# First attention: the weighted sum over the first key tile in three split passes, with half of the next queries in front of it

## The chip, the core and the metric

The kernel runs on one core of a Trainium2 chip. The metric is the time of one execution on the device in microseconds, as the median of several runs. The core has a matrix engine (PE, TensorE), a vector engine (DVE, VectorE), a scalar engine (ACT, ScalarE) and a general one (POOL, GpSimd). Each works off its own queue of instructions in order and waits for the others by semaphores. PE writes into PSUM, of which this kernel uses eight banks of 512 columns.

## What is computed

A block of six layers on x, 1024 tokens by 512: half a gated feed-forward layer, an attention, the same feed-forward layer again, then a low-rank feed-forward layer, a second attention and the low-rank layer again, each behind a layer norm and added to x. The change concerns the first attention. For each of 4 batches of 256 tokens it has 32 heads of width 128; a head's query is used twice, once on a key that four heads share and once on a latent key of its own:

```
q  = rope(x @ w_q)                 # 32 heads
k  = repeat(rope(x @ w_k), 4);  v  = repeat(x @ w_v, 4)
lk = rope((x @ w_lq) @ w_lk);   lv = x @ w_lv
attn = softmax(causal(q k^T * scale)) v
lat  = softmax(causal(q lk^T * scale)) lv
x = x + attn @ w_o + lat @ w_lo
```

All of it is in float32. The kernel gets float32's precision out of a reduced format (F32R) that PE reads faster: an operand is stored as a HI part, rounded to that format, and a LO part, the rest, and a product is made of three passes, HI x HI, HI x LO and LO x HI.

## The kernel before

`product` (L357 is its matmul) issues the three passes. A plain float32 matmul (both operands F32) is one instruction in the source and appears in the trace as two records, each with its own weight load.

The first attention runs over 8 groups of heads (one shared key each), and in a group over 16 steps: 4 batches of 4 query heads. A step handles two "instances": k = 0, the head on the shared key, and k = 1, the head on its latent key. That makes 128 steps and 256 instances. The groups 0 to 6 are a hardware loop, whose body starts with the step numbered 2; the last group is written out, without products for a next one. A step mixes three stages: the scores of step s, the turning and the weighted sum of step s-1, and the output product of step s-2. In it:

- PE (`a0_tensor_step`): `turn(0)` transposes the probabilities of instance 0 into bank PT (three blocks of 128x128: keys of tile 0 by queries of tile 0, keys of tile 0 by queries of tile 1, keys of tile 1 by queries of tile 1; the causal fourth block is empty). `scores` of both instances. In each third step of a batch (`st.key`) the next batch's keys. `weigh(0)`, the weighted sum into bank OB: a matmul over the first key tile for all 256 queries, and one over the second key tile for the last 128. `turn(1)`. `a0_queries`: twelve matmuls of 256 columns for the queries of two steps on, and three for their latent keys. `output(0)`: six matmuls of 512 columns. `weigh(1)`, `output(1)`. In each first step of a batch `a0_values` follows, 48 matmuls of 320 columns, four products of twelve.
- ACT (`a0_scalar_step`): `turned_out(0)` copies PT to `pt0` (L1086), the HI part of the last rotated query (L1070), the exponentials of both instances (L1079), `result_hi(0)` (the HI part of OB, L1091), `turned_out(1)`, HI parts of weight chunks (L256), the half swap of the queries for rope (L1064, L1065), `result_hi(1)`. In a key step the keys' swap stands between the exponentials of instance 0 and those of 1.
- DVE (`a0_vector_step`): the rotation of the last query (L1179, adds the cosine and the sine part), the row minima of both instances out of the scores' banks (L1191 for 128 columns, L1193 for 256), the inverses of the row sums (L1201), in a key step the key's cosine (L1170) and rotation, `result_lo(0)` (the LO part of OB, L1206), LO parts of weight chunks (L262), the queries' cosine (L1170), `result_lo(1)`, the output added to x (L1248, in each second step of a batch), and behind the values their four copies to `lvv` (L1213).
- POOL (`a0_gpsimd_step`): LO parts of the rotated queries and keys (L1286), the scaling of the probabilities by the inverses (L1297, L1299), the sine part of rope (L1278).

`weigh` waits until `a_pt` tells that its probabilities are in `pt0`, and until `a_o_lo` tells that OB has been emptied. `a0_claim` waits until the bank of a projection (two, in turn) has been released through `a_proj_free`.

Of the kernel before, what the change touches and what calls it, by code (L numbers as in the profile page):

```python
# [133 lines left out]
def program(nc, x_in, w_in, table_in, bias_in, rows_in, out):  # L134
    ctx = ExitStack()
    with ctx:
# [27 lines left out]
        with ExitStack() as a:  # L164
            xnB = [sb(a, f"xnB{i}", [P, KC, CH], F32R) for i in (HI, LO)]
            with ExitStack() as s:
                WF0 = [sb(s, f"WF0_{i}", [P, F0_CHUNKS * CH], F32R) for i in (HI, LO)]
                h0 = [sb(s, f"h0_{i}", [P, 2, CH], F32R) for i in (HI, LO)]
            with ExitStack() as s:

                qk = [sb(s, f"qk{i}", [P, 6, SEQ], F32R) for i in (HI, LO)]
                lvv = sb(s, "lvv", [P, 2, LVW])
                pt0 = sb(s, "pt0", [P, 2, 3 * P])
                oT0 = [sb(s, f"oT0_{i}", [P, 4, SEQ], F32R) for i in (HI, LO)]
                lqT = [sb(s, f"lqT{i}", [P, TOKENS], F32R) for i in (HI, LO)]
                s0 = sb(s, "s0", [P, 4, 3 * P])
                normed = sb(s, "normed", [P, 4, DIM])
# [597 lines left out]
        a_turned = sem("a_turned")  # L775
        a_pt = sem("a_pt")
        a_pv = sem("a_pv")
# [138 lines left out]
        def a0_queries(pe, st):  # L916

            dst, to = a0_claim(pe, st, "q"), st.near(2)
            for c in range(KC):
                w = (C_Q + to.h) * CH + c * P  # L920
                product(dst[:, 0:SEQ], lambda p: W[p][:, w:w + P],
                        lambda p: xn(p, c, to.tokens), c == 0, c == KC - 1)
            w = C_LK * CH + to.h * P
            product(dst[:, SEQ:2 * SEQ], lambda p: W[p][:, w:w + P],
                    lambda p: lqT[p][:, to.tokens]).then_inc(a_proj, 1)
# [17 lines left out]
        def a0_tensor_step(pe, st):  # L943
# [21 lines left out]
            def weigh(k):  # L965
# [3 lines left out]
                if before.h == 0 and k == 0:  # L969
# [102 lines left out]
        def a0_scalar_step(act, st):  # L1072
# [11 lines left out]
            def turned_out(k):  # L1084
                act.wait_ge(a_turned, before.inst(k)[0] + 1)
                nc.scalar.copy(pt0[:, k, :], bank[PT][:, 0:3 * P]).then_inc(a_pt, 1)  # L1086
# [13 lines left out]
            if st.key:  # L1100
                a0_swap(act, st, "k")
            if st.heads:
# [79 lines left out]
        def a0_vector_step(dve, st):  # L1182
# [25 lines left out]

            def values(i):
                tt, half = divmod(i, 2)  # L1210
                f, fs = st.fill(i)
                dve.wait_ge(a_proj, f + 1)
                nc.vector.tensor_copy(lvv[:, tt, half * HALF:(half + 1) * HALF],  # L1213
                                      bank[fs][:, 0:HALF]).then_inc(a_proj_free, 1)
# [9 lines left out]
            if st.first:  # L1224
                a0_cosine(dve, st, "q")
                values(0)
            if st.heads:
                inverses(0)
# [769 lines left out]
```

## Time and profile before

| | us |
|---|---|
| median of 3 runs | 1891.56 (1889.14 to 1893.09) |
| the profiled execution | 1892.9 |
| its span in the trace | 1891.1 |
| PE busy in the span | 1765.6 (93%) |
| DVE busy | 1124.1 (59%) |
| ACT busy | 1086.6 (57%) |
| POOL busy | 906.7 (48%) |

The steps of the first attention begin near 100 us and end near 1400 us, so they are more than two thirds of the span. The mean granted clock of TensorE over the span is 0.983 of full speed. In the timelines below a line is one instruction, or several of the same kind merged (x6), with start and duration in us; in brackets stands how long the engine had been idle before it and whose result ended that. A duration reaches to the end of the instruction; the next of the same engine may start before that.

### The profile page before, as it was taken

The numbers are of one execution on the slowest core, as the hardware profiler recorded it, in microseconds if no ns is written. First come the engines' busy times: TensorE is split into PE (matmuls) and PEld (weight loads), VectorE is DVE, ScalarE is ACT, GpSimd is POOL, SyncE is SP. The second block draws the span as 40 slices with busy tenths as digits, with TensorE's granted clock in tenths as the row PEclk, the third lists the DMA queues.
The fourth block names the chain that finished last, engine by engine and source line by source line (L and its number), as shares of the span: only waits on it lengthen the run. The fifth ranks groups of instructions, "written<-read, shape, count | busy, mean of one in ns | idle before, by whom it ended". The sixth has DMA issues, their size and how long they took to land.

```text
span 1891.1 us, 34627 instructions
## 1 busy us (share of the span) xinstructions
PE 1765.6 (93%) x11076; PEld 1530.7 (81%) x11076; DVE 1124.1 (59%) x3334; ACT 1086.6 (57%) x3071; POOL 906.7 (48%) x1153
## 2 busy tenths in 40 slices
PE   7979999999999999999999999999989788898788
PEld 5769988988998898898899989899968566666566
DVE  5655565556546546545655654664566767677656
ACT  3336565566547556556655655664642445777854
POOL 4445544555545455444555445454423326668720
PEclk9989999999999999999999999999989998999999
DMA  3300021012002101101200110110011200000001
GB/s 124 111 23 18 7 64 39 1 36 68 7 18 59 33 1 57 53 1 35 62 13 18 57 36 1 46 62 1 29 56 28 90 31 20 2 1 24 18 7 45
DMA packets 35462, 66.19 MB, mean 35 GB/s; under 512 B 4032, under 2 KB 4672, under 8 KB 35264
## 3 DMA queue, kind: packets, MB, share of 16 engines
q1 hardware_dynamic: 35264, 63.73, 11.0%
q8 instruction: 102, 1.67, 0.4%
q14 instruction: 96, 0.79, 0.1%
HBM read 61.62 MB, written 2.10 MB: 34 GB/s over the span
## 4 chain that ended last, share of the span: by engine, by line
PE 69%; DVE 9%; issue 8%; ACT 8%; POOL 5%; DMA 0%; DVEq 0%; SPq 0%; ACTq 0%; POOLq 0%
PE bank L357 54%; PE bank L974 5%; PE bank L961 4%; PE bank L976 3%; ACT s L1079 2%; POOL s L1795 1%; PE bank L1510 1%; PE bank L1481 1%; PE bank L1497 1%; DVE h L676 1%; POOL WF L269 1%; ACT s L1566 1%; ACT W L256 1%; POOL W L269 1%; POOL rstd L322 1%
## 5 line engine op out<-in xcount | busy, mean ns | idle before, releaser
L357 PE MATMUL bank<-W,oT 128*128 128x512 f32 x1632 | 433.2, 402 | 1.0 <-DVE oT L1747 1.0
L1286 POOL TENSOR_TENSOR qk<-work,qk 128x512 fp32r<-128x512 f32 (+1 forms) x160 | 191.5, 1197 | 469.0 <-ACT qk L1070 469.0
L357 PEld LDWEIGHTS bank<-W,oT 128*128 128x128 f32 x1632 | 290.3, 190 | 49.3 <-issue 1.3
L1086 ACT COPY pt<-bank 128x384 f32<-128x384 f32 x256 | 122.0, 477 | 338.8 <-PE bank L961 338.5
L1278 POOL TENSOR_TENSOR work<-work,table 128x512 f32<-128x512 f32 (+1 forms) x160 | 192.1, 1201 | 139.2 <-ACT work L1065 139.2
L1079 ACT ACTIVATE s<-s,neg_max 128x128 f32<-128x128 f32 (+1 forms) x512 | 227.7, 446 | 49.5 <-DVE neg_max L1193 48.7
L357 PE MATMUL bank<-W,xnA 128*128 128x320 f32 (+1 forms) x1056 | 186.5, 333 | 3.1 <-DVE xnA L342 2.8
L357 PEld LDWEIGHTS bank<-W,xnA 128*128 128x128 f32 x1056 | 166.9, 188 | 16.6 <-DVE xnA L342 4.0
L1170 DVE TENSOR_TENSOR work<-bank,table 128x512 f32<-128x512 f32 (+1 forms) x160 | 101.9, 637 | 128.7 <-ACT work L1065 128.7
L357 PE MATMUL bank<-xnA,W 128*128 128x256 f32 (+1 forms) x1080 | 162.7, 301 | 8.0 <-DVE W L262 6.6
L357 PE MATMUL bank<-xnB,W 128*128 128x256 f32 (+1 forms) x1080 | 165.9, 304 | 3.3 <-DVE xnB L342 3.3
L974 PE MATMUL bank<-pt,lvv 128*128 128x256 f32 x512 | 154.0, 382 | 14.9 <-DVE oT L1206 14.2
L357 PE MATMUL bank<-qk 128*128 128x256 f32 (+1 forms) x768 | 166.0, 351 | 0.0
L1213 DVE COPY lvv<-bank 128x320 f32<-128x320 f32 x128 | 62.9, 491 | 168.5 <-PE bank L357 168.5
L1299 POOL TENSOR_TENSOR s<-s,inv_sum 128x256 f32<-128x256 f32 x256 | 157.8, 616 | 0.0
L357 PEld LDWEIGHTS bank<-xnA,W 128*128 128x128 f32 x1080 | 143.3, 191 | 17.3 <-DVE W L262 9.6
L357 PEld LDWEIGHTS bank<-xnB,W 128*128 128x128 f32 x1080 | 146.0, 193 | 10.7 <-DVE xnB L342 4.0
L1795 POOL TENSOR_TENSOR s<-s,b_inv_sum 128x384 f32<-128x384 f32 x128 | 113.5, 907 | 61.7 <-DVE b_inv_sum L1714 61.5
L1179 DVE TENSOR_TENSOR work<-work 128x512 f32<-128x512 f32 (+1 forms) x160 | 116.0, 725 | 43.0 <-POOL work L1278 28.7
L1070 ACT CAST qk<-work 128x512 fp32r<-128x512 f32 (+1 forms) x160 | 92.3, 577 | 85.4 <-DVE work L1179 84.8
L961 PE MATMUL bank<-table,s 128*128 128x128 f32 x768 | 125.9, 273 | 10.4 <-issue 9.0
L1297 POOL TENSOR_TENSOR s<-s,inv_sum 128x128 f32<-128x128 f32 x256 | 108.0, 422 | 46.0 <-DVE inv_sum L1201 46.0
(106 smaller groups left out, 3516.7 us busy)
## 6 DMA issues: line engine op xcount, KB each, us to landing
raw<-in_weights SPq DMA_DIRECT2D x215, 256.0 KB, 2.8
x<-in_x SPq DMA_DIRECT2D x8, 256.0 KB, 5.9
out<-x SPq DMA_DIRECT2D x8, 256.0 KB, 2.1
row<-in_bias_rows SPq DMA_DIRECT2D x5, 256.0 KB, 2.7
table<-in_constants SPq DMA_DIRECT2D x4, 240.0 KB, 3.6
b_qk<-in_bias_rows SPq DMA_DIRECT2D x1, 512.0 KB, 3.8
b_val<-in_bias_rows SPq DMA_DIRECT2D x1, 256.0 KB, 3.0
table<-in_constants SPq DMA_DIRECT2D x1, 66.0 KB, 2.3
```

Of the source, the lines that this page charges most:

```text
L357: last = nc.tensor.matmul(out_ap, lhs(i), rhs(j), start=start and k == 0, stop=stop and k == 2)
L961: last = nc.tensor.transpose(bank[PT][:, blk * P:(blk + 1) * P], s0[:, s, blk * P:(blk + 1) * P], ident)
L974: nc.tensor.matmul(bank[OB][:, 0:SEQ], lvv[:, 0, col:col + P], pt0[:, k, 0:2 * P], start=True, stop=False)
L1079: last = nc.scalar.activation(s0[:, s, cols], s0[:, s, cols], ACT.Exp, bias=neg_max[:, s, qt:qt + 1], scale=-1.0, accum_out=row_sum[:, s, ...
L1086: nc.scalar.copy(pt0[:, k, :], bank[PT][:, 0:3 * P]).then_inc(a_pt, 1)
L1170: nc.vector.tensor_tensor(work[:, 2 + s, cols], bank[fs][:, cols], table[:, T_COS + cols.start:T_COS + cols.stop], ALU.mult).then_inc(a_pr ...
L1179: nc.vector.tensor_tensor(work[:, 2 + s, cols], work[:, 2 + s, cols], work[:, s, cols], ALU.add).then_inc(a_rope, 1)
L1278: nc.gpsimd.tensor_tensor(work[:, s, cols], work[:, s, cols], table[:, T_SIN + cols.start:T_SIN + cols.stop], ALU.mult).then_inc(a_sin, 1)
L1286: nc.gpsimd.tensor_tensor(lo, work[:, 2 + s, st.columns(what)], hi.bitcast(F32), ALU.subtract).then_inc(a_rope_lo, 1)
L1297: nc.gpsimd.tensor_tensor(s0[:, s, 0:P], s0[:, s, 0:P], inv_sum[:, s, 0:1].to_broadcast([P, P]), ALU.mult)
L1299: nc.gpsimd.tensor_tensor(s0[:, s, P:3 * P], s0[:, s, P:3 * P], inv_sum[:, s, 1:2].to_broadcast([P, 2 * P]), ALU.mult).then_inc(a_norm, 1)
L1795: nc.gpsimd.tensor_tensor(blocks, blocks, b_inv_sum[:, at, 1:4].unsqueeze(2).to_broadcast([P, 3, P]), ALU.mult).then_inc(b_norm, 1)
```

## The change

The weighted sum over the first key tile becomes a three-pass product of F32R parts; the one over the second key tile stays a plain float32 matmul.

- `lvv` (values of both key tiles, F32) becomes `lvv` HI and LO for the first tile and `lvv_late` (F32) for the second. ACT makes the HI part of the first two value products (`values_hi`, signalled by `a_val_hi`), and DVE makes their LO part in place of its copy; the other two remain DVE copies.
- `pt0` becomes `pt0` HI and LO of 256 columns for the first key tile and `pt0_late` of 128 for the second. ACT's `turned_out` writes the HI part of 256 columns only and signals `a_pt_hi`. On DVE a new `turned_lo(k)` waits for that, copies 128 columns to `pt0_late` and writes the LO part of 256 columns; `a_pt`, for which PE waits, is signalled by it. `turned_lo(0)` stands between the rotation of the last query and the minima, `turned_lo(1)` right behind `result_lo(0)`.
- PE: the first half of the queries' twelve matmuls, and the wait for their bank, go ahead of `weigh(0)`; the second half and the latent keys stay behind `turn(1)`.
- In the very first step `inverses(0)` on DVE comes ahead of the first value tile. `normed` gives its memory back, and `oT0` is placed over it.

```diff
-            def turned_out(k): ... nc.scalar.copy(pt0[:, k, :], bank[PT][:, 0:3 * P]).then_inc(a_pt, 1)
+                nc.scalar.copy(pt0[HI][:, k, :], bank[PT][:, 0:2 * P]).then_inc(a_pt_hi, 1)
...
+            def turned_lo(k):
+                n, _ = before.inst(k)
+                dve.wait_ge(a_pt_hi, n + 1)
+                nc.vector.tensor_copy(pt0_late[:, k, :], bank[PT][:, 2 * P:3 * P])
+                nc.vector.tensor_tensor(pt0[LO][:, k, :], bank[PT][:, 0:2 * P],
+                                        pt0[HI][:, k, :].bitcast(F32), ALU.subtract).then_inc(a_pt, 1)
...
                 pe.wait_ge(a_pt, n + 2)
                 pe.wait_ge(a_o_lo, n + 1)
-                nc.tensor.matmul(bank[OB][:, 0:SEQ], lvv[:, 0, col:col + P], pt0[:, k, 0:2 * P],
-                                 start=True, stop=False)
-                nc.tensor.matmul(bank[OB][:, P:SEQ], lvv[:, 1, col:col + P], pt0[:, k, 2 * P:3 * P],
+                product(bank[OB][:, 0:SEQ], lambda p: lvv[p][:, col:col + P],
+                        lambda p: pt0[p][:, k, :], True, False)
+                nc.tensor.matmul(bank[OB][:, P:SEQ], lvv_late[:, col:col + P], pt0_late[:, k, :],
                                  start=False, stop=True).then_inc(a_pv, 1)
...
+            if st.queries and not st.first:
+                a0_queries(pe, st, 0)
             if lag1:
                 weigh(0)
                 turn(1)
             if st.queries and not st.first:
-                a0_queries(pe, st)
+                a0_queries(pe, st, 1)
...
+            def values_hi(i):
+                act.wait_ge(a_proj, f + 1)
+                nc.scalar.copy(lvv[HI][:, i * HALF:(i + 1) * HALF],
+                               bank[fs][:, 0:HALF]).then_inc(a_val_hi, 1)
...
             if lagging(st):
                 result_hi(1)
+            if st.h == 0 and st.heads:
+                for i in range(1 if st.first else 0, 2):
+                    values_hi(i)
...
             if before.queries:
                 a0_rotate(dve, before, "q")
+            if lagging(st):
+                turned_lo(0)
             if st.heads:
                 minima(0)
                 minima(1)
...
             if lagging(st):
                 result_lo(0)
+                turned_lo(1)
```

## Rows read from the trace of the kernel before

**Rows 1.** The page: busy time by engine; one group of line 974.
```profile
PE 1765.6 (93%) x11076; PEld 1530.7 (81%) x11076; DVE 1124.1 (59%) x3334; ACT 1086.6 (57%) x3071; POOL 906.7 (48%) x1153
...
L974 PE MATMUL bank<-pt,lvv 128*128 128x256 f32 x512 | 154.0, 382 | 14.9 <-DVE oT L1206 14.2
```

**Rows 2.** Timeline of PE in an ordinary step: start, length, line, output<-inputs, count.
```profile
705.10 0.59 PE L974 MATMUL bank<-pt,lvv 128*128 128x256 f32 x2
705.53 0.38 PE L976 MATMUL bank<-pt,lvv 128*128 128x128 f32 x2
...
706.00 1.68 PE L357 MATMUL bank<-xnB,W 128*128 128x256 f32 x12
707.51 0.52 PE L357 MATMUL bank<-lqT,W 128*128 128x256 f32 x3
...
709.26 0.59 PE L974 MATMUL bank<-pt,lvv 128*128 128x256 f32 x2
...
712.69 0.59 PE L974 MATMUL bank<-pt,lvv 128*128 128x256 f32 x2
```

**Rows 3.** Timeline of DVE in the same step.
```profile
704.03 0.69 DVE L1179 TENSOR_TENSOR work<-work 128x512 f32<-128x512 f32 x1 [0.44 <-POOL work L1278]
705.45 0.29 DVE L1191 CUSTOM_DVE_ANT_0 s<-bank,table 128x128 f32<-128x128 f32 x1 [0.73 <-PE bank L357]
...
705.67 0.42 DVE L1193 CUSTOM_DVE_ANT_0 s<-bank,table 128x256 f32<-128x256 f32 x1
...
708.29 0.42 DVE L1206 TENSOR_TENSOR oT<-bank,oT 128x256 fp32r<-128x256 f32 x1
```

**Rows 4.** Timeline of ACT in the same step.
```profile
704.24 0.48 ACT L1086 COPY pt<-bank 128x384 f32<-128x384 f32 x1 [1.31 <-PE bank L961]
...
707.41 0.50 ACT L1079 ACTIVATE s<-s,neg_max 128x256 f32<-128x256 f32 x1
...
707.90 0.35 ACT L1091 CAST oT<-bank 128x256 fp32r<-128x256 f32 x1
708.16 0.47 ACT L1086 COPY pt<-bank 128x384 f32<-128x384 f32 x1
```

**Rows 5.** Timeline of DVE where a batch's last value copy meets the next step.
```profile
726.13 0.49 DVE L1213 COPY lvv<-bank 128x320 f32<-128x320 f32 x1 [1.27 <-PE bank L357]
726.53 0.68 DVE L1179 TENSOR_TENSOR work<-work 128x512 f32<-128x512 f32 x1
727.67 0.29 DVE L1191 CUSTOM_DVE_ANT_0 s<-bank,table 128x128 f32<-128x128 f32 x1 [0.45 <-PE bank L357]
```

**Rows 6.** Timelines of DVE, ACT and PE in a key step, put together.
```profile
696.42 0.29 DVE L1191 CUSTOM_DVE_ANT_0 s<-bank,table 128x128 f32<-128x128 f32 x1 [0.24 <-PE bank L357]
...
700.82 0.41 DVE L1206 TENSOR_TENSOR oT<-bank,oT 128x256 fp32r<-128x256 f32 x1
...
697.51 0.49 ACT L1079 ACTIVATE s<-s,neg_max 128x256 f32<-128x256 f32 x1
...
698.12 0.37 ACT L1064 COPY work<-bank 64x256 f32<-64x256 f32 x1
...
701.67 0.59 PE L974 MATMUL bank<-pt,lvv 128*128 128x256 f32 x2
```

**Rows 7.** Timelines of DVE and PE in the first step behind the loop's turn.
```profile
782.61 0.41 DVE L1206 TENSOR_TENSOR oT<-bank,oT 128x256 fp32r<-128x256 f32 x1
...
783.16 0.67 PE L974 MATMUL bank<-pt,lvv 128*128 128x256 f32 x2 [0.70 <-DVE oT L1206]
```

**Rows 8.** Timelines of DVE and PE in a key step with a weight split.
```profile
735.24 0.68 DVE L262 TENSOR_TENSOR W<-raw,W 128x512 fp32r<-128x512 f32 x1
735.84 0.69 DVE L1179 TENSOR_TENSOR work<-work 128x512 f32<-128x512 f32 x1
736.44 0.29 DVE L1191 CUSTOM_DVE_ANT_0 s<-bank,table 128x128 f32<-128x128 f32 x1
...
735.98 1.69 PE L357 MATMUL bank<-xnA,W 128*128 128x256 f32 x12 [0.94 <-DVE W L262]
```

More of the change, by code:

```diff
@@ L171, in program @@
                 qk = [sb(s, f"qk{i}", [P, 6, SEQ], F32R) for i in (HI, LO)]
-                lvv = sb(s, "lvv", [P, 2, LVW])
-                pt0 = sb(s, "pt0", [P, 2, 3 * P])
-                oT0 = [sb(s, f"oT0_{i}", [P, 4, SEQ], F32R) for i in (HI, LO)]
+                lvv = [sb(s, f"lvv{i}", [P, LVW], F32R) for i in (HI, LO)]
+                lvv_late = sb(s, "lvv_late", [P, LVW])
+                pt0 = [sb(s, f"pt0_{i}", [P, 2, 2 * P], F32R) for i in (HI, LO)]
+                pt0_late = sb(s, "pt0_late", [P, 2, P])
                 lqT = [sb(s, f"lqT{i}", [P, TOKENS], F32R) for i in (HI, LO)]
                 s0 = sb(s, "s0", [P, 4, 3 * P])
-                normed = sb(s, "normed", [P, 4, DIM])
+                with ExitStack() as entry:
+                    normed = sb(entry, "normed", [P, 4, DIM])
+                oT0 = [sb(s, f"oT0_{i}", [P, 4, SEQ], F32R) for i in (HI, LO)]
             with ExitStack() as s:
@@ L914, in a0_keys, with a0_queries @@
             last.then_inc(a_proj, 1)
-        def a0_queries(pe, st):
-            dst, to = a0_claim(pe, st, "q"), st.near(2)
-            for c in range(KC):
+        def a0_queries(pe, st, part=None):
+            to = st.near(2)
+            if part != 1:
+                a0_claim(pe, st, "q")
+            dst = bank[st.fill("q")[1]]
+            for c in range(KC) if part is None else range(2 * part, 2 * part + 2):
                 w = (C_Q + to.h) * CH + c * P
@@ L922, in a0_queries @@
                         lambda p: xn(p, c, to.tokens), c == 0, c == KC - 1)
+            if part == 0:
+                return
             w = C_LK * CH + to.h * P
@@ L1085, in turned_out @@
                 act.wait_ge(a_turned, before.inst(k)[0] + 1)
[L1086 removed]
+                nc.scalar.copy(pt0[HI][:, k, :], bank[PT][:, 0:2 * P]).then_inc(a_pt_hi, 1)
+            def values_hi(i):
+                f, fs = st.fill(i)
+                act.wait_ge(a_proj, f + 1)
+                nc.scalar.copy(lvv[HI][:, i * HALF:(i + 1) * HALF],
+                               bank[fs][:, 0:HALF]).then_inc(a_val_hi, 1)
             def result_hi(k):
@@ L1101, in a0_scalar_step @@
                 a0_swap(act, st, "k")
+            if st.first:
+                values_hi(0)
             if st.heads:
@@ L1211, in values @@
                 f, fs = st.fill(i)
-                dve.wait_ge(a_proj, f + 1)
-                nc.vector.tensor_copy(lvv[:, tt, half * HALF:(half + 1) * HALF],
-                                      bank[fs][:, 0:HALF]).then_inc(a_proj_free, 1)
+                cols = slice(half * HALF, (half + 1) * HALF)
+                if tt == 0:
+                    dve.wait_ge(a_val_hi, st.g * (2 * BATCH) + (2 * st.batch + i + 1))
+                    nc.vector.tensor_tensor(lvv[LO][:, cols], bank[fs][:, 0:HALF],
+                                            lvv[HI][:, cols].bitcast(F32),
+                                            ALU.subtract).then_inc(a_proj_free, 1)
+                else:
+                    dve.wait_ge(a_proj, f + 1)
+                    nc.vector.tensor_copy(lvv_late[:, cols], bank[fs][:, 0:HALF]).then_inc(a_proj_free, 1)
             turn_of = None if st.last_group else st.g
@@ L1225, in a0_vector_step @@
                 a0_cosine(dve, st, "q")
+            if st.heads:
+                inverses(0)
+            if st.first:
                 values(0)
             if st.heads:
-                inverses(0)
                 inverses(1)
```

2 lines of the change are left out of this document (added).

## The prediction, made before the changed kernel was run

> **What bounds the kernel now.** I read the page first: PE is busy 93% of the span, DVE and ACT are near 60% [rows 1]; PE also makes up most of the chain that ended last. The first attention is 128 steps of two heads each; the plain product of `weigh` is issued in two halves per sum, so 512 records of one line are 256 sums, two a step. Then I read one ordinary step engine by engine. PE runs from scores to scores without a hole: first sum at 705.10, second at 709.26, the next step's first sum 7.59 us after this one's [rows 2]. So work taken from PE is worth its length, as long as nothing that PE waits for comes later than its turn. How near is the second sum's input? A step has one fixed chain: the scores end, DVE takes the minima from 705.45, ACT the exponentials back to back up to 707.90, then ACT empties the first sum (`result_hi`, 707.90) and copies the turned probabilities (`turned_out`, 708.16, ends 708.63) [rows 3, 4]. PE uses that copy at 709.26: 0.63 us later. The first sum of a step uses a copy that ends at 704.72, 0.38 us ahead of its use. That is all the cover that a longer hand-over has.
>
> **The change part by part.** (1) The 256-column product costs 0.43 us now (705.10 to 705.53). The three passes have the form of the queries' twelve, 1.51 us, or 0.126 each [rows 2]: 0.378. It saves 0.055 a sum, 0.11 a step, 256 x 0.055 = 14 us if all of it counts. If three passes took as long as the one product, that is rival D. The 128-column product is kept.
>
> (2) Each probability tile gets a second stage. ACT's copy shrinks from 384 to 256 columns: like `result_hi` it takes 0.35 to 0.37 instead of 0.47, 0.11 earlier. Behind it DVE copies 128 columns and subtracts 256. No DVE copy of 128 columns stands in the trace. The 320-column copy takes 0.49 and lets the next start after 0.40 [rows 5]; the minimum over 128 columns takes 0.29 and lets its successor start after 0.22 [rows 3]. I take 0.20, near the second row; bounds are 0.16 (0.40 x 128/320) and 0.29 (no overlap). The subtraction is `result_lo`'s form, 0.42, next start after 0.33 [rows 3]. So the stage is 0.62 long and takes 0.53 of DVE's time.
> The Trainium skill's page "VectorE: DVE Perf Modes", section "The DRAIN you can't avoid", speaks against such a split: the next operation starts only when the pipe is empty. With 0.29 + 0.42 the stage would be 0.71 and the forecast some 8 us later. The rows show successors 0.08 us before the end of the one ahead [rows 3, 5], so my sum goes by them.
>
> (3) First sum. `turned_lo(0)` stands behind the rotation (704.03; it lets the next start 0.60 later, 735.84 to 736.44 [rows 8]) and ahead of the minima. In the ordinary step it runs 704.63 to 705.25 and frees DVE at 705.17, before the minima at 705.45: hidden. After the values, the last copy at 726.13 pushes the rotation to 726.53 and the minima to 727.67 [rows 5]: 726.53 + 0.60 + 0.53 = 727.66, just hidden. PE needs the tile 0.15 us after DVE's end (782.61 + 0.41 = 783.02, sum at 783.16 [rows 7]): 705.40, where PE would be at 705.10. The moved half of the queries, 0.75 us, brings it to 705.85, so no stall; without it there would be one of 0.3. The half itself costs nothing, it is the same work in another place, and its bank was released by a value copy or a cosine over 1 us before.
>
> (4) Second sum, ordinary step. ACT ends at 708.16 + 0.36 = 708.52, DVE is in `result_lo(0)` from 708.29 and free at 708.63; copy to 708.83, subtraction to 709.25, PE at 709.40. PE would like it at 709.26 - 0.055 = 709.20. The sum starts 0.14 later than now, and with its own 0.055 saved the step is 0.08 longer, not 0.11 shorter. The moved queries don't help here, since the chain starts at the scores and PE's work between scores and second sum is the same. Bounds: the copy's 0.16 and 0.29, and for PE's start 0.06 behind a DVE weight split (735.98 after 735.92 [rows 8]), so -0.05 and +0.17. Some 58 steps are of this kind: +5 (-3 to +10). In 14 more, just ahead of a wait of PE that is there already, it is absorbed.
>
> (5) Key steps. DVE has less room: it is idle 0.24 us before the minima at 696.42, and 0.08 more by the overlap of neighbours; `turned_lo(0)` takes 0.53, so they start 0.21 later. ACT waits there for the keys anyway (the exponential at 697.51 lets the next start after 0.49, at 698.00; the swap starts at 698.12), so 0.09 of it reaches the swap, the second exponentials, the rotation of the key and `result_lo(0)`, 700.82 [rows 6]. Then 700.91 + 0.33 + 0.20 + 0.42 + 0.15 = 702.01 against 701.67: +0.34, less 0.055 = +0.28. (In other words: 0.09 + 0.53 behind `result_lo`, of which 701.67 - 700.82 - 0.41 - 0.15 = 0.29 is free.) 16 steps: +4.5.
>
> (6) Where DVE is already last, all of it counts. At six loop turns DVE starts late, the minima follow the rotation at once, and PE waits for `result_lo(0)`, 0.70 us in the one shown [rows 7]: +0.53 from the first stage, +0.20 + 0.33 + 0.02 from the second, less 0.055: +1.03 each, with the last group's such step (0.8, where PE only just doesn't wait yet) +7. In the key step with PE's 0.94 us wait for a weight split, the minima at 736.44 follow the rotation at once too: +0.53 [rows 8], of which ACT's wait for the keys eats 0.11, and 0.53 - 0.29 behind `result_lo` as in (5), less 0.055: +0.61, seven times, +4.3. In the steps behind these two kinds DVE comes late to the rotation from two weight splits, so the minima again follow at once and the ordinary 0.14 is on top: 0.53 + 0.14 - 0.055 = 0.6 behind the split steps (seven), 0.5 behind the loop's turn (seven), and 0.3 one step further (seven), where half of the delay has faded: +10. Most of the 14.2 us that PE waited for `result_lo` [rows 1] lies in the last three steps: +1.0, +1.0 and +0.7, with 1.5 for the first two steps, which have no output products to cover: +4.
>
> (7) The value tiles: two of four copies become an ACT copy (about 0.42) and a DVE subtraction (0.49), ACT has nothing else to do in a batch's value stretch; behind its new waits stand only late weight casts and the next step's copies, which need a later product of PE anyway, and a bank is wanted only a whole value product after its own ended. Nothing, and up to +0.5 once in the first step, where ACT has exponentials behind it. Released memory and the later place of one buffer: nothing.
>
> Sum: 5 + 4.5 + 7 + 4.3 + 10 + 4 = 35. The profiled execution took 1892.9 us (span 1891.1, 1.8 around it), 1.3 above the median 1891.56. 1891.6 + 34.8 = 1926.
>
> **The rivals.** (A) PE stays the bound and the extra stage is hidden everywhere: 1891.6 - 14 = 1878. For it: DVE is idle 40% of the time, PE is busy 93%. Against it: the idle time lies elsewhere than between 708.63 and 709.26. It would need 0.2 us less than my rows give in each ordinary step. This is the one on the other side.
> (B) The ordinary step just makes it, the special ones don't: 58 x -0.11 = -6 in place of +5, and half the key steps' price: 34.8 - 11 - 2 = 22, 1913. It decides at a DVE stage shorter by 0.2 us, or PE using the data 0.1 earlier.
> (C) `turned_lo(0)` isn't hidden before the minima in ordinary steps either. If the rotation, which waits for POOL's sine, or ACT's copy comes some tenths later, each 0.1 us in 58 to 72 steps is 6 to 7 us; a full 0.3 makes 1946. For it: zero room after the values and 0.09 in others.
> (D) The saved length isn't there (three passes as slow as the one product): where the chain sets the time only the second sum's 0.055 was counted, in some 110 steps: 6 us, 1932, inside the forecast.
>
> **How the numbers follow.** Forecast (1916 to 1942, D within) 0.62; B (1898 to 1916) 0.14; A 0.13; C beyond 1942 0.11. A is all "faster"; B may end near no change. This kernel's runs can't tell 0.2%, 3.8 us, from nothing. Faster 0.14, same 0.05, slower 0.81. The range leaves A and the far end of C out and takes the bounds of the unknown costs in: 1896 to 1946.
>
> **What would show it.** Right: ordinary step about 7.67 us instead of 7.59, a new idle of PE before the second sum of every step, released by the DVE subtraction; none before the first sum; loop-turn steps with 1.7 us instead of 0.70 before the second sum; three passes in about 0.38. Wrong: steps of 7.48 (A), minima later against the scores (C), or PE idle before the first sum. It would also be wrong if the longer instruction stream changed the engines' late start at the loop's turn, whose cause nothing here shows.

## The result, and the profile after

| | before | after |
|---|---|---|
| median, us | 1890.35 (4 runs) | 1928.63 (1926.93 to 1932.48, 4 runs) |
| ratio, after to before | | 1.0197 (95% interval 1.0178 to 1.0217) |
| the profiled execution's span | 1891.1 | 1929.8 (the slowest of the four) |
| mean granted clock of TensorE | 0.983 | 0.977 |

The change costs 38 us, 2.0%. The forecast was 1926, slower.

The page of the changed kernel: busy time by engine, and the group of the three passes (L360 is `product` now). The columns of a group are line, engine, operation, output<-inputs, shape, count | busy us, mean ns | idle before it and what ended most of it.

```profile
PE 1787.2 (93%) x11332; PEld 1526.1 (79%) x11332; DVE 1248.1 (65%) x3846; ACT 1089.8 (56%) x3135; POOL 913.0 (47%) x1153
...
L360 PE MATMUL bank<-pt,lvv 128*128 128x256 f32 x768 | 148.2, 302 | 23.9 <-DVE pt L1236 22.4
```

DVE has 124 us more to do and is still idle a third of the time, as its share says. PE's busy share hasn't moved at all. Neither says where the 38 us are. An ordinary step does (PE, then DVE, then ACT; L1235 and L1236 are `turned_lo`, L1098 is `turned_out`):

```profile
720.98 0.52 PE L360 MATMUL bank<-pt,lvv 128*128 128x256 f32 x3
721.34 0.39 PE L986 MATMUL bank<-pt_late,lvv_late 128*128 128x128 f32 x2
...
722.97 1.55 PE L360 MATMUL bank<-W,oT 128*128 128x512 f32 x6
724.47 0.62 PE L360 MATMUL bank<-pt,lvv 128*128 128x256 f32 x3
724.93 0.39 PE L986 MATMUL bank<-pt_late,lvv_late 128*128 128x128 f32 x2
...
728.63 0.52 PE L360 MATMUL bank<-pt,lvv 128*128 128x256 f32 x3
```
```profile
719.83 0.29 DVE L1235 COPY pt_late<-bank 128x128 f32<-128x128 f32 x1
720.04 0.41 DVE L1236 TENSOR_TENSOR pt<-bank,pt 128x256 fp32r<-128x256 f32 x1
720.63 0.29 DVE L1214 CUSTOM_DVE_ANT_0 s<-bank,table 128x128 f32<-128x128 f32 x1 [0.18 <-PE bank L360]
...
723.46 0.42 DVE L1229 TENSOR_TENSOR oT<-bank,oT 128x256 fp32r<-128x256 f32 x1
723.80 0.28 DVE L1235 COPY pt_late<-bank 128x128 f32<-128x128 f32 x1
724.00 0.41 DVE L1236 TENSOR_TENSOR pt<-bank,pt 128x256 fp32r<-128x256 f32 x1
```
```profile
723.08 0.35 ACT L1109 CAST oT<-bank 128x256 fp32r<-128x256 f32 x1
723.33 0.36 ACT L1098 CAST pt<-bank 128x256 fp32r<-128x256 f32 x1
```

From first sum to first sum it is 7.65 us, where [rows 2] gave 7.59. The first sum doesn't wait: its tile is ready at 720.04 + 0.41 = 720.45, PE takes it at 720.98, and the minima still wait for PE (0.18 us idle). The second sum's tile is ready at 724.00 + 0.41 = 724.41, and PE starts at 724.47, 0.06 later: it waited for this one. The wait is so short that the records of pipelined matmuls overlap it and no idle time is printed. It shows in the output product ahead, from whose start to the sum's it is 1.50 us (722.97 to 724.47), where it was 1.39 before the change:

```profile
707.87 1.55 PE L357 MATMUL bank<-W,oT 128*128 128x512 f32 x6
709.26 0.59 PE L974 MATMUL bank<-pt,lvv 128*128 128x256 f32 x2
```

And it costs a second time, behind the start: the three passes of the sum that waited take 0.46 to the next product's start (724.47 to 724.93), those of the first sum, which didn't wait, 0.36. So in the second sum the three passes are slower than the one product, which took 0.43.

Step lengths over the whole attention, from the first transpose of a step to that of the next, sorted by kind. The kinds are those of the prediction; a group's steps are numbered 2 to 17, "split" are the steps with two weight splits on DVE beside the keys.

| steps (number of them) | before, us | after, us | change, sum | forecast |
|---|---|---|---|---|
| ordinary (49) | 7.59, 14.6 with values | +0.064 each | +3.1 | } +5 |
| ordinary, step 9 of a group (7) | 7.59 | +0.43 each | +3.0 | } |
| step 13, ahead of PE's wait for a split (8) | 7.58 | +0.07 each | +0.5 | 0 |
| key (16) | 9.02 | +0.365 each | +5.8 | +4.5 |
| split key step 14 (7) | 10.22 | +0.53 each | +3.7 | +4.3 |
| step 15 (7), 3 (8), 16 (7) | | +0.33, +0.25, +0.35 | +6.8 | +10 |
| loop's turn: steps 17 and 2 (14) | | +1.38, +0.31 | +11.8 | +7 |
| first two and last steps | | | -1.0 | +4 |
| all | | | +33.7 | +34.8 |

The span grew by 38.7; the rest (5 us) lies behind the first attention, whose code is untouched. From profile to profile of these kernels the stretch from the last step's first transpose to the end took 497 to 508 us, without order. I count it as scatter of single executions, not as an effect.

The page's list of waits, PE's part in the first attention, before and after (engine, line <- whom: us in total, times, longest):

```profile
PE bank L974 <- DVE oT L1206: 14.2, 10, 4.5
PE bank L961 <- issue: 9.0, 6, 1.7
```
```profile
PE bank L360 <- DVE pt L1236: 20.7, 37, 3.2
PE bank L971 <- issue: 18.1, 6, 3.2
```

Three things: PE now waits for `turned_lo`, its 14.2 us of waiting for `result_lo` are gone, and its idle at the six loop turns doubled. The last was not in the forecast's sum.

### The profile page after: what moved, and what is told of

The parts are those of the page before. It is cut to its first block, busy times and chain, and to the rows that moved or that the text cites. A ratio compares the mean times of both kernels' runs of the same rounds, so it can differ in the third digit from the quotient of the medians.

```text
span 1929.8 us, 35759 instructions
## 1 busy us (share of the span) xinstructions
PE 1787.2 (93%) x11332; PEld 1526.1 (79%) x11332; DVE 1248.1 (65%) x3846; ACT 1089.8 (56%) x3135; POOL 913.0 (47%) x1153
## 4 chain that ended last, share of the span: by engine, by line
PE 50%; ACT 16%; DVE 15%; issue 12%; POOL 6%; DMA 0%; DVEq 0%; SPq 0%; ACTq 0%; POOLq 0%
PE bank L360 42%; ACT s L1091 5%; PE bank L971 2%; PE bank L986 2%; DVE pt L1236 2%; POOL work L1319 2%; ACT work L1077 2%; ACT W L259 2%; ACT work L1076 2%; POOL s L1836 1%; DVE work L1202 1%; PE bank L1522 1%; ACT s L1607 1%; PE bank L1551 1%; DVE pt_late L1235 1%
## 5 line engine op out<-in xcount | busy, mean ns | idle before, releaser
L360 PE MATMUL bank<-W,oT 128*128 128x512 f32 x1632 | 435.1, 403 | 1.0 <-DVE oT L1788 1.0
L360 PEld LDWEIGHTS bank<-W,oT 128*128 128x128 f32 x1632 | 291.6, 191 | 51.0 <-issue 1.5
L1098 ACT CAST pt<-bank 128x256 fp32r<-128x256 f32 x256 | 94.7, 370 | 229.5 <-PE bank L971 229.5
L360 PE MATMUL bank<-W,xnA 128*128 128x320 f32 (+1 forms) x1056 | 186.5, 333 | 4.0 <-DVE xnA L345 2.8
L360 PEld LDWEIGHTS bank<-W,xnA 128*128 128x128 f32 x1056 | 166.6, 188 | 17.8 <-DVE xnA L345 4.0
L360 PE MATMUL bank<-xnA,W 128*128 128x256 f32 (+1 forms) x1080 | 174.3, 306 | 6.8 <-DVE W L265 5.4
L360 PE MATMUL bank<-xnB,W 128*128 128x256 f32 (+1 forms) x1080 | 170.7, 301 | 3.2 <-DVE xnB L345 3.2
L360 PEld LDWEIGHTS bank<-xnA,W 128*128 128x128 f32 x1080 | 154.4, 197 | 20.6 <-DVE W L265 8.4
L360 PE MATMUL bank<-pt,lvv 128*128 128x256 f32 x768 | 148.2, 302 | 23.9 <-DVE pt L1236 22.4
L360 PEld LDWEIGHTS bank<-pt,lvv 128*128 128x128 f32 x768 | 108.2, 189 | 77.4 <-DVE pt L1236 74.6
L360 PE MATMUL bank<-qk 128*128 128x256 f32 (+1 forms) x768 | 168.7, 356 | 0.0
L360 PEld LDWEIGHTS bank<-xnB,W 128*128 128x128 f32 x1080 | 150.6, 191 | 14.6 <-DVE xnB L345 4.0
```

The costliest lines, as they stand in the source:

```text
L360: last = nc.tensor.matmul(out_ap, lhs(i), rhs(j), start=start and k == 0, stop=stop and k == 2)
L1098: nc.scalar.copy(pt0[HI][:, k, :], bank[PT][:, 0:2 * P]).then_inc(a_pt_hi, 1)
```

## The experiments

The theory: PE waits in every step for the second sum's tile, at the end of the chain scores, minima, exponentials of both instances, `result_hi(0)`, `turned_out(1)`, `result_lo(0)`, `turned_lo(1)`. Rivals: the three passes cost what they should save; DVE's load as such; the moved queries; the loop's longer code. Each ratio is to the kernel before on the same chip. Its median there was 1893.0 for the kernels `after_order`, `before_order`, `after_queries_whole` and `before_half`, 1894.4 for the four with `act_late` or `quarter` in their names, and 1893.7 for the other four.

**What PE's saving is worth alone.** The kernel before with the three passes; the LO parts are left out. (`lvv` and `pt0` also get the reduced format, and the product over the second key tile reads them as float32.)

```diff
-                nc.tensor.matmul(bank[OB][:, 0:SEQ], lvv[:, 0, col:col + P], pt0[:, k, 0:2 * P],
-                                 start=True, stop=False)
+                product(bank[OB][:, 0:SEQ], lambda p: lvv[:, 0, col:col + P],
+                        lambda p: pt0[:, k, 0:2 * P], True, False)
```

> The kernel before with three passes in the first key tile's product and nothing of the second stage: ACT's one copy rounds all 384 columns, and all three passes use the HI parts. It leaves the LO parts of the probabilities and values out. It shows what PE's saving is worth with nothing behind it. Theory: ordinary steps 7.44 to 7.48 us instead of 7.59 (0.055 to 0.076 a sum), 1872 to 1879 us. Rival (three passes are not cheaper, the step length comes from them): 1889 to 1900. The idle of PE at the loop's turn tells whether the longer PE stream of the loop's body lengthens it: by that theory to 3 us, which takes back 9 us.

Measured: 1876.7 us, ratio 0.9912 (0.9878 to 0.9945). The chain is as before the change and ordinary steps take 7.43 us (697.19 to 704.62):

```profile
697.19 0.49 PE L961 MATMUL bank<-table,s 128*128 128x128 f32 x3
...
698.57 0.52 PE L357 MATMUL bank<-pt,lvv 128*128 128x256 f32 x3
698.92 0.39 PE L976 MATMUL bank<-pt,lvv 128*128 128x128 f32 x2
...
704.62 0.49 PE L961 MATMUL bank<-table,s 128*128 128x128 f32 x3
```

The passes take 0.35 where the one product took 0.43: 0.08 a sum. So the saving is real and larger than forecast. Between this and the changed kernel an ordinary step differs by 0.22 us: 0.12 is the wait before the second sum, 0.10 the longer passes behind it (0.46 for 0.35). PE's idle at the loop's turns rose only from 1.2 to 1.65 us (before) to 1.6 to 1.9, so the longer code explains a small part of the 3 us.

**The chain by itself, made 0.20 us longer.**

```diff
             def turned_lo(k):
...
+                if k == 1:
+                    nc.vector.tensor_copy(spare[:, before.s % 2, :], bank[PT][:, 2 * P:3 * P])
                 nc.vector.tensor_copy(pt0_late[:, k, :], bank[PT][:, 2 * P:3 * P])
```

> The changed kernel with one more DVE copy of 128 columns (0.28 long, 0.20 of DVE's time) in front of turned_lo(1), into a buffer that nobody reads. It prices the disputed chain by itself. Theory (every step waits for the DVE stage ahead of the second sum): nearly every step gets 0.20 us longer, ordinary steps 7.85 us instead of 7.65, 112 x 0.20 = 22 us in all, 1948 to 1954 us. Rival (the DVE stage is not what PE waits for; the loss is elsewhere): DVE is busy 65% of the time and hides 26 us more, 1928 to 1933.

Measured: 1947.5 us, ratio 1.0292 (1.0261 to 1.0324), some 18 us above the changed kernel and just under what I expected. Its ordinary step, from transpose to transpose, is 7.84 us, with PE again 0.06 us behind DVE's end (731.48 + 0.41 = 731.89, 731.95):

```profile
726.18 0.49 PE L972 MATMUL bank<-table,s 128*128 128x128 f32 x3
...
731.95 0.62 PE L361 MATMUL bank<-pt,lvv 128*128 128x256 f32 x3
...
734.02 0.49 PE L972 MATMUL bank<-table,s 128*128 128x128 f32 x3
```
```profile
731.09 0.28 DVE L1237 COPY spare<-bank 128x128 f32<-128x128 f32 x1
731.28 0.28 DVE L1238 COPY pt_late<-bank 128x128 f32<-128x128 f32 x1
731.48 0.41 DVE L1239 TENSOR_TENSOR pt<-bank,pt 128x256 fp32r<-128x256 f32 x1
```

In ordinary and in key steps 0.20 us more on the chain is 0.20 us more per step (7.65 to 7.86 and 9.38 to 9.58 on average); an engine that is idle a third of the time hid none of it there. The split key steps did hide it (10.75 and 10.74), and the ninth step of a group even got shorter (8.01 to 7.85), so the sum is 18 us and not 128 times 0.20.

**The chain made shorter.** The copy goes to ACT, ahead of the HI part.

```diff
             def turned_out(k):
...
+                nc.scalar.copy(pt0_late[:, k, :], bank[PT][:, 2 * P:3 * P])
                 nc.scalar.copy(pt0[HI][:, k, :], bank[PT][:, 0:2 * P]).then_inc(a_pt_hi, 1)
...
             def turned_lo(k):
-                nc.vector.tensor_copy(pt0_late[:, k, :], bank[PT][:, 2 * P:3 * P])
```

> The changed kernel with its 128-column copy given to ACT, ahead of the copy of the HI part, so that DVE's stage is the subtraction alone (0.33 of its time instead of 0.53). Nothing is left out. Theory (the size of the hand-over sets the step): ACT's two copies start at the present place and end about 0.15 to 0.2 us later than the one did, DVE's subtraction follows at once instead of behind a copy, so the tile is ready 0.05 to 0.1 us earlier than after the change; ordinary steps 7.55 to 7.60 us instead of 7.65, and the steps in which DVE is late gain 0.2: 1908 to 1918 us. Rival (DVE's stage doesn't matter, ACT's time does): same or slower, 1928 to 1945.

Measured: 1906.0 us, ratio 1.0060 (1.0034 to 1.0087), 1.3% better than the change and 2 us better than expected. ACT's second copy costs 0.15 us (717.03 to 717.18, the next start), DVE's cost 0.20. Ordinary steps take 7.54 us, 0.10 less:

```profile
717.59 0.42 DVE L1236 TENSOR_TENSOR pt<-bank,pt 128x256 fp32r<-128x256 f32 x1
```
```profile
718.07 0.61 PE L360 MATMUL bank<-pt,lvv 128*128 128x256 f32 x3
```

The tile is ready at 717.59 + 0.42 = 718.01, and PE starts 0.06 later, which is only 0.02 us later than without any wait (from the last matmul ahead to the sum it is 0.246 us on average, against 0.227 where PE doesn't wait). Even so the passes take 0.46 (718.07 to 718.53). That is why the step isn't at 7.43: a wait of 0.02 us costs 0.12.

**The minima later.** `turned_lo(0)` ahead of the rotation.

```diff
+            if lagging(st):
+                turned_lo(0)
             if before.queries:
                 a0_rotate(dve, before, "q")
-            if lagging(st):
-                turned_lo(0)
```

> The changed kernel with turned_lo(0) ahead of the rotation on DVE instead of behind it. Theory (the chain to the second sum starts at the minima, so what delays them delays PE): in ordinary steps turned_lo(0) has to wait for ACT's copy at 0.6 us behind the rotation's present start, so rotation and minima come some 0.3 us later and steps get up to 0.3 us longer: 1938 to 1960 us. Behind weight splits it helps. Rival (the minima have room): 1920 to 1930.

Measured: 1954.6 us, ratio 1.0328 (1.0295 to 1.0360). Ordinary steps take 7.96 us (731.40 to 739.36). The copy waits 1.23 us for ACT, rotation and minima follow without a gap, and the second sum carries it:

```profile
732.33 0.29 DVE L1235 COPY pt_late<-bank 128x128 f32<-128x128 f32 x1 [1.23 <-ACT pt L1098]
732.54 0.41 DVE L1236 TENSOR_TENSOR pt<-bank,pt 128x256 fp32r<-128x256 f32 x1
732.87 0.68 DVE L1202 TENSOR_TENSOR work<-work 128x512 f32<-128x512 f32 x1
733.47 0.28 DVE L1214 CUSTOM_DVE_ANT_0 s<-bank,table 128x128 f32<-128x128 f32 x1
```
```profile
737.30 0.62 PE L360 MATMUL bank<-pt,lvv 128*128 128x256 f32 x3 [0.28 <-DVE pt L1236]
```

This is rival C, provoked: some 25 us for 0.3 us a step. In the changed kernel's ordinary steps it doesn't happen, as the minima wait for PE there.

**The queries.** Whole behind `turn(1)` in the changed kernel; and the half moved in front in the kernel before.

```diff
-            if st.queries and not st.first:
-                a0_queries(pe, st, 0)
             if lag1:
                 weigh(0)
                 turn(1)
             if st.queries and not st.first:
-                a0_queries(pe, st, 1)
+                a0_queries(pe, st)
```

> The changed kernel with the half of the queries back behind turn(1). Theory: turned_lo(0) ends some 0.2 to 0.5 us after PE wants the first sum, so a wait appears there in three of four steps; the wait before the second sum shrinks by as much as it can (0.1 us), so these 96 steps become 0.1 to 0.4 us longer: 1945 to 1960 us. Rival (only the second sum's chain, which starts at the scores, sets a step): no change, 1925 to 1932.

> The kernel before with the half of the queries put in front of the first sum, nothing else. Theory: the same PE work in another order with nothing late: 1889 to 1893 us, ordinary steps 7.59 us. It also tells whether the longer idle of PE at the loop's turn (2.8 to 3.2 us after the change, 1.2 to 1.65 before) comes with the moved queries: by my theory not, it stays near 1.5 us. Rival: it rises to 3 us here, and the time to 1900.

Measured: 1943.1 us, ratio 1.0257 (1.0233 to 1.0281), and 1893.8 us, ratio 1.0005 (0.9987 to 1.0024). Without the moved half the first sum follows DVE's end (727.25 + 0.41 = 727.66) by 0.06:

```profile
726.36 1.30 PE L360 MATMUL bank<-qk 128*128 128x256 f32 x6
727.72 0.62 PE L360 MATMUL bank<-pt,lvv 128*128 128x256 f32 x3
```
```profile
727.05 0.29 DVE L1233 COPY pt_late<-bank 128x128 f32<-128x128 f32 x1
727.25 0.41 DVE L1234 TENSOR_TENSOR pt<-bank,pt 128x256 fp32r<-128x256 f32 x1
```

The step is 7.76 us, 0.11 longer than with the half in front; behind the values it is more (8.05). 1943 is just under what I expected. The moved half is worth 11 us (by the ratios) to 15 us (by the medians) to this change and nothing (0.05%) to the kernel before: it covers the first sum, as the prediction said, and can't help the second. It doesn't lengthen the loop's turn by itself either (1.2 to 1.6 us in the kernel before with the half moved).

**Taking work out of the chain.** The exponentials of instance 1 don't feed the second sum, but ACT ran them ahead of what does.

```diff
 (ACT)
-            if st.heads:
-                exponentials(1)
             if lagging(st):
                 result_hi(0)
                 turned_out(1)
+            if st.heads:
+                exponentials(1)
...
 (DVE)
                 inverses(0)
...
+            if lagging(st):
+                result_lo(0)
+                turned_lo(1)
             if st.heads:
                 inverses(1)
...
-            if lagging(st):
-                result_lo(0)
-                turned_lo(1)
```

> The changed kernel with one order altered: ACT does result_hi(0) and turned_out(1) ahead of the exponentials of instance 1, DVE does result_lo(0) and turned_lo(1) ahead of inverses(1). Nothing is left out. Theory (the second sum waits for a chain scores, minima, exponentials, result, copy, DVE stage, that is some 0.2 us too long): the exponentials of instance 1, 0.88 us, leave that chain, PE no longer waits before the second sum, ordinary steps take 7.48 us instead of 7.65, and the saved 14 us of the three passes come out; the waits for result_lo behind the loop's turn and in the last steps shrink too, so 1865 to 1885 us. Rival (the three passes, or DVE's 5% more load as such, are what costs): the order moves a few us only, 1915 to 1930.

> The kernel before with the same altered order (result_hi(0) and turned_out(1) ahead of the exponentials of instance 1, result_lo(0) ahead of inverses(1)). Theory: in ordinary steps PE waits for nothing, so they stay at 7.59 us; only the waits for result_lo behind the six loop turns (0.7 to 1.4 us each) and in the last steps (4.47 and 3.40 us) shrink: 1876 to 1884 us. Rival (the order itself disturbs other chains, as the scaling on POOL comes 0.5 us later): no gain or slower, 1888 to 1900.

Measured: 1898.6 us, ratio 1.0032 (1.0018 to 1.0046), and 1890.6 us, ratio 0.9987 (0.9970 to 1.0003). Both missed the numbers; `before_order` came out where its rival had it. The ordinary steps did what I expected (-0.15 and 0.00 against before, but for the eleventh of a group, 0.17 longer in `after_order`), the key steps too (-0.15 and 0.00). But the step behind the loop's first one got 1.4 us longer and the one behind the other splits 0.86. There DVE and PE show (in `after_order`):

```profile
631.24 0.69 DVE L1202 TENSOR_TENSOR work<-work 128x512 f32<-128x512 f32 x1 [0.77 <-POOL work L1319]
631.85 0.28 DVE L1235 COPY pt_late<-bank 128x128 f32<-128x128 f32 x1
```
```profile
632.51 0.62 PE L360 MATMUL bank<-pt,lvv 128*128 128x256 f32 x3 [1.44 <-DVE pt L1236]
```

The inverses of instance 1 come later, so POOL's scaling of that instance runs beside DVE's two weight splits and takes 0.54 and 1.06 us, where that of instance 0 took 0.40 and 0.61. Its sine comes late, the rotation waits for the sine, and `turned_lo(0)` waits behind the rotation in DVE's queue, though it doesn't need it. So with the new order `turned_lo(0)` belongs ahead of the rotation, the edit that alone had cost 25 us. In `before_order` the step behind the loop's first one got longer too (7.60 to 8.39); PE's idle at the loop's turns fell to 0.2 to 0.8 us, and the profiled attention is 5 us shorter, but what lies behind it 5 us longer.

> after_order (exponentials and inverses of instance 1 behind the second tile's hand-over) with turned_lo(0) also ahead of the rotation. Nothing is left out. Theory: with the exponentials of instance 1 off the chain there are 0.7 us of room, so minima 0.3 us later cost nothing, and the waits of PE for turned_lo(0) behind a late rotation (1.4 us in the second step behind the loop's turn, 0.9 behind the other split steps), which took back 17 us in after_order, go away: 1880 to 1886 us, faster than both kernels. Rival (these waits come from something else, such as POOL's late work): 1895 to 1900.

Measured: 1886.5 us, ratio 0.9969 (0.9949 to 0.9989): 0.3% below the kernel before, with an interval that leaves out 1, and 2.2% below the changed one. Its ordinary step is 7.43 us; the second tile is ready at 701.07 + 0.41 = 701.48, 0.49 us ahead of PE:

```profile
701.07 0.41 DVE L1236 TENSOR_TENSOR pt<-bank,pt 128x256 fp32r<-128x256 f32 x1
```
```profile
701.97 0.52 PE L360 MATMUL bank<-pt,lvv 128*128 128x256 f32 x3
```

**Variants of it.** With the ACT copy of `act_late`, without and with `turned_lo(0)` ahead; and with a quarter of the queries in front instead of a half (the chunks of part 0 are `(0,)`, of part 1 `(1, 2, 3)`).

> act_late together with the order of after_order. Theory: ordinary steps 7.43 us as in after_order, and the waits behind late rotations shrink by the 0.2 us that turned_lo(0) is shorter: 1888 to 1896 us. Rival: ACT's 0.2 us more per tile makes the weight casts late, 1898 to 1905.

> act_late_order with turned_lo(0) ahead of the rotation. Theory: as after_order_ahead (1886 us), with 0.2 us less of DVE in front of each minimum: ordinary steps 7.43 us still, the seven steps behind weight splits a little shorter: 1880 to 1887 us. Rival: ACT becomes late in the split steps, 1888 to 1895.

> after_order_ahead with only a quarter of the queries (three matmuls, 0.38 us) in front of the first sum. Theory: the first tile is ready 0.2 us after PE's earliest wish, so a quarter covers it and ordinary steps stay at 7.43 us: 1884 to 1889 us. It also tells whether PE's longer idle at the loop's turn (2.3 to 2.75 us there, 1.3 to 1.7 with the queries whole) goes with how much is moved: if so, it falls to about 2 us; if it doesn't, its cause stays open.

Measured: 1896.4 us, ratio 1.0015 (1.0002 to 1.0027); 1893.7 us, ratio 0.9991 (0.9978 to 1.0005); 1887.9 us, ratio 0.9964 (0.9949 to 0.9979). The first is at the upper edge of what I expected, the second missed it and lies where its rival had it, the third is as expected. In the first two, ordinary steps are at 7.43 us, so there is nothing left for a shorter stage to win there. Against `after_order_ahead`, moving the copy to ACT costs 0.1 to 0.4 us in each of the steps 3, 14 and 16 of a group, those with weight splits or behind them: the rival that I had written down against it. A quarter of the queries covers the first sum as well as a half.

**PE's idle at the loop's six turns**, us, in the order of time:

```
before               1.58 1.20 1.65 1.61 1.35 1.57
before_three_passes  1.64 1.63 1.59 1.94 1.93 1.70
before_half          1.59 1.21 1.33 1.40 1.48 1.21
before_order         0.81 0.69 0.21 0.27 0.53 0.69
after                2.92 3.19 2.75 3.16 2.88 3.21
after_queries_whole  1.36 1.49 2.54 1.73 1.26 1.50
after_ahead          2.67 3.12 2.95 3.13 3.18 2.88
after_copy_twice     2.77 2.70 2.51 2.75 2.12 2.17
act_late             2.92 2.71 3.37 1.58 3.05 2.95
after_order          1.05 1.21 1.05 2.44 1.44 1.26
act_late_order       2.44 2.52 2.18 0.97 0.86 1.12
after_order_ahead    2.32 2.68 2.64 2.75 2.59 2.60
act_late_order_ahead 1.21 1.40 2.25 2.46 2.65 1.47
.._quarter           1.49 1.50 2.37 2.88 2.50 1.59
```

Neither the passes nor the moved queries alone bring the long idle. Both together don't always bring it either: `after_order` has both and the short idle at five of six turns, and in six kernels it jumps from turn to turn. With the queries whole the changed kernel runs the same number of PE instructions as with the half in front and has the short idle at five of six turns, so it isn't the length of PE's code.

The DMA records of the same traces show what it goes with. Queue q8 carries instructions, in pages of 16 KB. In the 5 us before the fourth turn, before and after the change (columns: pages, MB, share of the 16 engines' time):

```profile
q8 instruction: 1, 0.02, 1.5%
```
```profile
q8 instruction: 2, 0.03, 4.7%
```

In the 38 turns of the table in which the last two pages start within 1.4 us of each other PE idles 2.18 to 3.37 us; in the other 46 they start 2.18 us apart or more, and it idles 0.21 to 2.17. In all 84, PE goes on 1.6 to 2.5 us behind the landing of the last page. So the idle goes with the loading of instructions. That the loading is its cause, and what brings two pages together, isn't shown: no kernel here was built to test it.

## Why the prediction was right, and where it wasn't

The time, the sign and the main mechanism held: 1928.6 against a forecast of 1926, and 33.7 us in the steps against 34.8; PE waits for the new stage before the second sum of every step but four. That the two sums agree so closely is partly luck: the terms are off by up to 5 us each, in both directions, and at the loop's turn the mechanism was another. Point by point:

- *Second sum, ordinary step* (part 4). Forecast 0.08 us longer, measured 0.064. Two terms were off and cancelled. PE starts 0.06 us behind DVE's subtraction, not 0.15, so that, counted from the scores, the sum starts 0.03 later than before the change (5.33 for 5.30) and not 0.14. I had both values for the start in the rows ([rows 7] and [rows 8]) and took the longer. And behind their wait the three passes take 0.46, 0.03 more than the plain product, where I had them 0.055 shorter; that a short wait lengthens what stands behind it was no term of my sum. Where PE doesn't wait they take 0.35 to 0.36, not 0.378, so the saving there is 0.08 a sum, 20 us if all 256 had it and not 14. The first sums have it where PE doesn't wait for them; the second sums, of which all but four wait, have none.
- *The DVE stage* (part 2). Copy 0.29 long with the next start after 0.20, subtraction 0.41: as taken. The Trainium skill, "VectorE: DVE Perf Modes", section "The DRAIN you can't avoid", says that the next operation doesn't start until the pipe is empty, and in the same paragraph that one which isn't held starts earlier; the prediction used the first half only. The trace agrees with the second: the subtraction starts 0.20 us behind the start of a copy of 0.28 (723.80 to 724.00).
- *First sum* (part 3). Covered in ordinary and key steps, and the price without the moved half was 11 to 15 us more in the experiment. In most of the steps 3, 15 and 16 PE does wait for it, by less than 0.1 us, and its passes take 0.46 (the tile comes late behind the weight splits); in the last two steps it waits longer, see below.
- *Key steps* (part 5). 0.365 instead of 0.28. The sum starts 0.34 later than before, as forecast (but `result_lo(0)` came 0.1 later than I had it and PE took the tile 0.09 sooner); the rest is again the passes behind the wait, 0.03 more than the plain product and not 0.055 less. The second tile's stage in the key step:

```profile
715.83 0.41 DVE L1229 TENSOR_TENSOR oT<-bank,oT 128x256 fp32r<-128x256 f32 x1
716.16 0.28 DVE L1235 COPY pt_late<-bank 128x128 f32<-128x128 f32 x1
716.36 0.41 DVE L1236 TENSOR_TENSOR pt<-bank,pt 128x256 fp32r<-128x256 f32 x1
```
```profile
716.82 0.62 PE L360 MATMUL bank<-pt,lvv 128*128 128x256 f32 x3 [0.26 <-DVE pt L1236]
```

- *Split steps* (part 6). 0.53 instead of 0.61, and the steps behind them 0.25 to 0.35 instead of 0.3 to 0.6: I let the delay fade too slowly.
- *Loop's turn* (part 6). The step that failed: 11.8 us against 7, and by another mechanism. I added 1.03 us to each for `turned_lo`, on top of an unchanged start, and had PE wait 1.7 us for DVE behind it. In fact PE itself started later, 9.1 us over the six turns, and DVE was no longer late against it: the 5.4 us of waiting for `result_lo` that followed these turns before the change are gone; for `turned_lo` PE waits in two of them only, 0.2 us each. What made the rest is the clock of TensorE, which was at its full level of 2.4 GHz around all six turns before the change. Steps 17 and 2 together, turn by turn:

| turn | PE's idle, before and after | both steps, before and after | granted clock after |
|---|---|---|---|
| 1 | 1.58, 2.92 | 19.83, 19.94 | 1.00 |
| 2 | 1.20, 3.19 | 19.21, 22.54 | 0.85 |
| 3 | 1.65, 2.75 | 19.45, 19.78 | 1.00 |
| 4 | 1.61, 3.16 | 19.35, 22.37 | 0.85 |
| 5 | 1.35, 2.88 | 19.58, 21.13 | 0.92 |
| 6 | 1.57, 3.21 | 19.12, 21.44 | 0.92 |

  Where the clock stayed up, the turn cost 0.1 and 0.3 us, a fraction of the forecast's 1.03; where it fell to the lower level for a while, behind the long idle, 1.6 to 3.3. PE's busy time in these two steps, with the same instructions, rose from 17.0 to 18.2 and to 19.3 us there, 7.2 us over the four turns. The same two steps of the last group, ahead of which no loop turns, add 1.2 us, where I had 0.8. The windows of the first two turns, and the 9 us around the fourth, in which the scores took 2.27 us instead of 1.29:

```profile
291.58:311.52 19.94, 16.96 (x112) 14.65 (x110) 14.29 (x44) 13.08 (x37) 10.53 (x14) 1.00 0.17 48
454.51:477.05 22.54, 19.35 (x113) 17.22 (x110) 14.73 (x45) 13.00 (x37) 10.82 (x14) 0.85 0.17 46
```
```profile
791.00:800.00 9.00, 6.53 (x31) 6.27 (x32) 3.61 (x14) 2.91 (x9) 1.52 (x2) 0.62 0.20 66
```
```profile
793.47 0.87 PE L971 MATMUL bank<-table,s 128*128 128x128 f32 x3 [3.16 <-issue]
794.00 2.27 PE L360 MATMUL bank<-qk 128*128 128x256 f32 x6
```

  (Columns of a window: length, busy us of PE, its weight loads, DVE, ACT, POOL, granted clock, share of DMA, GB/s.) The prediction named a later start at the turn as what would make it wrong; it was wrong there, and terms that were too high elsewhere made up for it.
- *First and last steps.* Forecast +4, measured -1. PE's long waits before the second sums of the last steps shrank from 4.47 and 3.40 us to 1.58 and 3.18, since PE now stops before the first sums of these steps too, for 1.89 and 0.71 us: `turned_lo(0)` stands behind a weight split and the rotation in one and behind layer norm work in the other.

```profile
1406.27 0.71 PE L360 MATMUL bank<-pt,lvv 128*128 128x256 f32 x3 [1.89 <-DVE pt L1236]
```

  So these steps have waits before the first sum, which the prediction named as a sign of being wrong. The clock was kinder here: 0.86 over these two steps, where it had been 0.75, and the sums behind the long waits took 0.62 us, where they had taken 1.19.
- *Seven ordinary steps* (the ninth of a group) got 0.43 us longer instead of 0.06, with DVE held 0.27 us by nothing that the trace shows, between `turned_lo(0)` and the minima. On a chain without slack such a hole is paid by PE.
- *The rivals.* A is out: its 0.2 us of room didn't exist, as the kernels with the chain 0.20 longer and 0.1 shorter show. B is out with it. C doesn't happen here and costs some 25 us where it does. D is half right: where PE doesn't wait, the passes save more than forecast, but in the waiting second sums they are as slow as the one product (0.46 against 0.43). Its 1932 lay inside the forecast.

So the expected gain was there, 17 us as measured with the passes alone. It was given back, and more, by a new wait that ends the chain of nearly every step, by what the wait costs behind it, and by the clock at four loop turns. `after_order_ahead` gets 7 of the 17 us: its ordinary and key steps have all of the saving. Where the other 10 go its profile can't show, as it is of the fastest of ten runs, and that of `before_three_passes` of the slowest of four; their attention is equally long (1249 us). The ten runs lie in the order of their clock: 1880.5 to 1882.8 us at a granted clock of 0.981 to 0.984, 1890.6 to 1893.2 at 0.974 to 0.976.

## What to carry to other kernels

Before shortening the busiest engine's work, measure for each thing it waits for by how much the thing is early, and compare that with what the edit adds to the hand-over; here 0.4 us of room met 0.5 us of new stage in every ordinary step. A miss by 0.02 us is dear too, as it cost 0.12 in `act_late`. An idle share says nothing about this: 0.20 us more on an engine that is idle a third of the time cost 0.20 us in every ordinary step. If the room is missing, look in the in-order queues ahead of the hand-over for work that doesn't feed it; and try such edits together, since one that cost 25 us alone was worth 12 us behind another.

## What the runs showed of the hardware that I had not expected

- Three passes of 256 columns in the reduced format take 0.35 to 0.36 us, 0.12 each, when PE doesn't wait before them; the plain float32 product of the same size takes 0.43. The 0.126 of the run of twelve is an average that depends on what stands ahead: half of it takes 0.71 us behind the scores (720.27 to 720.98) and 0.80 behind transposes (721.81 to 722.61).
- The same three passes take 0.46 us when PE had to wait before them, whether the wait was 0.02 us (`act_late`), 0.12 (the changed kernel) or 0.4 (its key steps).
- A wait of PE of 0.1 us leaves no idle time in its records, nor does one of 0.3 (`after_copy_twice`, 731.95). It shows in the length of the step, and in the start of the waiting matmul, 0.05 to 0.06 us behind the end of DVE's instruction in every ordinary and key step with such a wait.
- PE's idle at the loop's turn lies between 0.2 and 3.4 us in these kernels, and goes with how close together pages of instructions are loaded. Behind four of the changed kernel's six turns (idle 2.9 to 3.2 us) the clock fell to its lower level, behind two (2.8 and 2.9) and behind all six of the kernel before (1.2 to 1.7) it didn't.
